# Conditional residual matmul on one core: VectorE multiplies half of the masks in while it evicts, and the first unit's x comes staged

## The chip, the cores and the metric

One Trainium2 chip, one of its cores. The time is the device time of one execution in microseconds (us), lower is better. All data is float32.

## The reference, cut to what matters

```python
# x (128, 128, 512), y = cond_8 (128, 8), weight (8, 512, 512), mask (512, 512), bias (512,)
masked_w = weight * mask[None, :, :]
w_bot = jnp.einsum('bg,got->bot', y, masked_w)      # one 512x512 matrix for each batch b
x = x + jnp.einsum('bnt,bot->bno', x, w_bot) + bias
```

Each of the 128 batches has its own matrix `w_bot[b]`, a sum of eight masked matrices weighted by `y[b]`. It is made on the chip, then multiplied with `x[b]`, and the input and a bias are added.

## The kernel before

**Units.** The work is cut into 8 units: 2 slices of 256 output columns, times 4 windows of 32 batches. A unit has 16 bursts (16 output rows `o` of the mask each), which make `w_bot` of its window and slice in `wbot`, and jobs, which multiply x with `wbot` and leave sums in a PSUM bank. 16 groups of 2 batches make up a unit. While a unit's jobs run, the bursts of the next unit run between them; only the first 8 bursts of the program (`HALF`) stand alone at the start.

**A burst** (`burst(b)`, L528) is 16 matmuls, 4 row tiles `j` by 4 parts `k` of t. The stationary operand is `wm`, weights that were multiplied by the mask; the moving one is `y_sb`, a blocked table of y. Row tiles run beside each other on 32 rows of the array each. Each row tile fills a bank of its own. Each of these four tiles is evicted from PSUM to its place in `wbot`: ScalarE takes tiles 0 and 2 (`ACT.Copy`, L363), VectorE tiles 1 and 3 (`tensor_copy`, L440), by `on_vector` (L156).

**x itself.** In unit 0 the residual x is added by TensorE: each burst has four further bf16 matmuls (`add_x`, L539) of the 0/1 table `eye_sb`, which add the identity to `w_bot`. `AHEAD` says which bursts have them first and which last. In the other units x comes from DRAM a second time, laid out like the output (`xn`), into the six buffers `staged`; VectorE adds the bias to it (L458) and then the sums (`add_sums`, L476). In unit 0 `add_sums` adds the bias straight to the sums.

**Masks.** The weights of a slice lie in `wm`, 16 blocks of 256 KB, and each block is multiplied by an equally large block of mask (`multiply_mask`, L278): for slice 0 by VectorE for blocks 0, 1 and 3 and by GpSimd (POOL) for the others, for slice 1 by POOL alone, while units 2 and 3 run. Masks of slice 0 lie where later x groups go (`first_mask`), so an x group waits for the multiplications that read its place (`masked`, L271). POOL's order is that of the blocks.

**Queues.** SyncE (SP) issues nearly every load in one written order: 8 blocks of weights and masks, two x groups, then pairs of blocks between x groups; later an x group as soon as its ring place is free, `xn` as soon as an output buffer is stored, and from x group 48+2 on the weights and masks of slice 1 (`LOAD_W_AT`). ScalarE's queue issues the first mask, y, the 0/1 table, the bias and all stores. `room` (L515) makes TensorE wait until its bank was evicted (`s_ev_v`, `s_ev_a`) or its sums were added (`s_o`).

**Jobs.** The first jobs of a unit are pieces of all 128 rows (`piece`, L584). Later groups come four jobs at a time in four turns (`turn`, L597) with a burst between turns. In the first half of unit 0 a job takes half of the columns, and two bursts stand ahead of jobs 2, 4, 6 and 7. The banks go round: the third and fourth tile of burst 9 take the banks of job 0 and job 1, so they wait for VectorE's `add_sums` of these.

## Time and profile before

| what | value |
|---|---|
| time, median of 3 runs | 588.47 us (587.61 to 588.82) |
| time of the profiled execution | 590.58 us |
| its span | 588.8 us |
| TensorE (PE) busy | 577.1 us, 98% of the span |
| VectorE (DVE) busy | 328.7 us, 56% |
| ScalarE (ACT) busy | 160.5 us, 27% |
| GpSimd (POOL) busy | 38.4 us, 7% |
| loads and stores | 148.71 MB, 253 GB/s over the span |

The profiled execution took 1.8 us more than its span and 2.1 us more than the median of the three timed runs. A line of the profile names an engine, the line of the kernel, what is written and what is read. PEld is TensorE's weight load, which runs beside the matmuls. A float32 matmul has two records of each kind, so a burst shows as x32, and a turn of 16 matmuls as x32.

### The profile page before, as it was taken

Reading aid. Unit: us, or ns where it says so; the run is one execution under the profiler, and the core shown is the slowest. Engines: PE = TensorE matmul, PEld = TensorE weight load, DVE = VectorE, ACT = ScalarE, POOL = GpSimd, SP = SyncE. Lnnn points to the kernel's source line nnn. Section 1 sums busy time; section 2 is a strip of 40 time slices with the busy share of each in tenths; the row PEclk is TensorE's granted clock in tenths of the full one; section 3 lists DMA queues with packets and bytes.
Section 4 is the critical chain, followed back from the end, with each engine's and each line's share of the span. In section 5 each row is a group of like instructions: output and inputs, shape, how many; then the busy total and the mean of one; then the engine's idle time right before and its main releaser. Section 6 shows DMA issues by size and latency. Waiting matters only on the chain.

```text
span 588.8 us, 20669 instructions
## 1 busy us (share of the span) xinstructions
PE 577.1 (98%) x9148; PEld 542.0 (92%) x9148; DVE 328.7 (56%) x600; ACT 160.5 (27%) x334; POOL 38.4 (7%) x34
## 2 busy tenths in 40 slices
PE   7899999999999999999999999999999999999998
PEld 4799999889998999989899899998999989999887
DVE  5562557346673476645666356663566635665333
ACT  5340444014440144302343023430234203441000
POOL 3430000000000011123110000000000000000000
PEclk9999999999999999999999999999999999999999
DMA  9978546884668869899676875769676795759842
GB/s 320 407 298 287 179 147 216 288 332 154 220 216 306 282 199 326 264 351 411 244 269 223 313 267 164 258 187 349 201 216 212 226 339 185 243 172 313 273 159 89
DMA packets 59849, 148.71 MB, mean 253 GB/s; under 512 B 6624, under 2 KB 7520, under 8 KB 59760
## 3 DMA queue, kind: packets, MB, share of 16 engines
q1 hardware_dynamic: 40176, 113.00, 57.4%
q10 hardware_dynamic: 19584, 34.39, 15.4%
q8 instruction: 72, 1.18, 0.8%
q14 instruction: 17, 0.14, 0.1%
HBM read 113.81 MB, written 33.55 MB: 250 GB/s over the span
## 4 chain that ended last, share of the span: by engine, by line
PE 96%; DMA 1%; issue 1%; POOL 1%; SPq 1%; DVE 0%; DVEq 0%; POOLq 0%
PE ps L592 43%; PE ps L611 34%; PE ps L562 19%; DMA xs<-in_mask 1%; POOL wm L284 1%; SPq L307 0%; SPq L313 0%; PE ps L545 0%; DVE wbot L440 0%; DVE staged L476 0%; DVEq L474 0%; POOLq L282 0%
## 5 line engine op out<-in xcount | busy, mean ns | idle before, releaser
L592 PE MATMUL ps<-wbot,xs 128*128 128x256 f32 (+1 forms) x1400 | 253.7, 343 | 0.8 <-DVE wbot L440 0.8
L592 PEld LDWEIGHTS ps<-wbot,xs 128*128 128x128 f32 x1400 | 227.1, 191 | 25.4 <-issue 1.6
L363 ACT ACTIVATE wbot<-ps 128x512 f32<-128x512 f32 (+2 forms) x277 | 140.8, 567 | 343.0 <-PE ps L562 337.1
L611 PE MATMUL ps<-wbot,xs 32*128 32x256 f32 x3584 | 220.9, 376 | 0.1
L440 DVE COPY wbot<-ps 128x512 f32<-128x512 f32 (+2 forms) x274 | 164.6, 646 | 93.2 <-PE ps L562 89.6
L611 PEld LDWEIGHTS ps<-wbot,xs 32*128 32x128 f32 x3584 | 188.1, 185 | 2.6 <-issue 1.0
L562 PEld LDWEIGHTS ps<-y_sb,wm 32*128 32x128 f32 x4096 | 144.8, 186 | 11.4 <-issue 7.0
L562 PE MATMUL ps<-y_sb,wm 32*128 32x128 f32 x4096 | 147.9, 273 | 5.9 <-issue 4.3
L476 DVE TENSOR_TENSOR staged<-ps,staged 128x256 f32<-128x256 f32 (+2 forms) x121 | 63.9, 544 | 140.5 <-PE ps L592 127.2
L458 DVE TENSOR_TENSOR staged<-staged,bias_sb 128x512 f32<-128x512 f32 (+2 forms) x121 | 79.3, 661 | 0.0
L284 POOL TENSOR_TENSOR wm<-wm,mask_sb 128x512 f32<-128x512 f32 x16 | 21.3, 1354 | 243.4 <-DMA mask_sb<-in_mask 243.4
L400 ACT ACTIVATE eye_sb<-ps 128x256 f32<-128x256 f32 x56 | 18.5, 381 | 25.1 <-PE ps L611 25.1
L476 DVE TENSOR_TENSOR staged<-ps,bias_sb 128x256 f32<-128x256 f32 x24 | 9.8, 423 | 19.2 <-PE ps L592 15.7
L476 DVE TENSOR_TENSOR staged<-eye_sb,staged 128x256 f32<-128x256 f32 x48 | 18.0, 417 | 0.1
L284 POOL TENSOR_TENSOR wm<-wm,xs 128x512 f32<-128x512 f32 x13 | 16.4, 1271 | 21.9 <-DMA xs<-in_mask 21.8
L619 PE MATMUL ps<-staged 128*128 128x512 f32 x4 | 3.6, 1047 | 1.4 <-DVE staged L478 1.4
L545 PE MATMUL ps<-eye_sb 32*128 32x128 bf16 x64 | 3.6, 219 | 1.0 <-DMA eye_sb<-in_eye 0.8
L284 DVE TENSOR_TENSOR wm<-wm,xs 128x512 f32<-128x512 f32 x3 | 2.1, 689 | 4.1 <-DMA xs<-in_mask 4.1
L545 PEld LDWEIGHTS ps<-eye_sb 32*128 32x128 bf16 x64 | 1.8, 93 | 2.2 <-DMA eye_sb<-in_eye 1.0
L619 PEld LDWEIGHTS ps<-staged 128*128 128x128 f32 x4 | 1.2, 324 | 2.5 <-DVE staged L478 1.4
L476 DVE TENSOR_TENSOR staged<-eye_sb,bias_sb 128x256 f32<-128x256 f32 x8 | 3.0, 417 | 0.0
L363 ACT ACT_TABLE_LOAD x1 | 1.3, 1283 | 3.2 <-issue 3.2
(6 smaller groups left out, 1.5 us busy)
## 6 DMA issues: line engine op xcount, KB each, us to landing
xs<-in_x SPq DMA_DIRECT2D x128, 512.0 KB, 5.4
out<-staged ACTq DMA_DIRECT2D x127, 256.0 KB, 5.1
staged<-in_xn SPq DMA_DIRECT2D x112, 256.0 KB, 3.9
wm<-in_w SPq DMA_DIRECT2D x12, 512.0 KB, 8.5
mask_sb<-in_mask SPq DMA_DIRECT2D x8, 512.0 KB, 7.5
wm<-in_w SPq DMA_DIRECT2D x8, 256.0 KB, 5.9
xs<-in_mask SPq DMA_DIRECT2D x4, 512.0 KB, 13.0
xs<-in_mask SPq DMA_DIRECT2D x7, 256.0 KB, 6.3
```

The lines of the kernel that those rows point to most:

```text
L284: return eng.tensor_tensor(wm[:, c, :], wm[:, c, :], by, ALU.mult)
L363: eng.activation(tile_place(b, j, first, end), tile_sums(b, j, first, end), ACT.Copy).then_inc(s_ev_a, 1)
L400: eng.activation(late_of(i), ps[BANK_OF[i, None]][:, 0:SL], ACT.Copy).then_inc(s_late, 1)
L440: eng.tensor_copy(tile_place(b, j, first, end), tile_sums(b, j, first, end)).then_inc(s_ev_v, 1)
L458: ins = eng.tensor_tensor(at, at, bias_of(i, at.shape[1]), ALU.add)
L476: eng.tensor_tensor(at, total, at if m >= OWN_X else bias_of(i, at.shape[1]), ALU.add).then_inc(s_o, 1)
L545: ins = eng.matmul(bank[j][:, own * P:(own + 1) * P], eye_sb[rows[j], c % (P // CO), :], ones_sb[rows[j], :], start=ahead, stop=behind)
L562: ins = eng.matmul(bank[j][:, k * P:(k + 1) * P], wm[rows[j], c, k * P:(k + 1) * P], y_sb[rows[j], win, :], start=not (ahead and k == own) ...
L592: ins = eng.matmul(bank[:, at:at + width], group[:, h, k, :], sums_of(slice(0, P), u, g, h, c, end, k), start=(k == 0), stop=(k == KT - 1))
L611: ins = eng.matmul(ps[BANK_OF[i, None]][:, 0:WIDTH[i]], xs[rows, X_AT[u, g] % XRING, h, k, :], sums_of(rows, u, g, h, c, end, k), start=(n ...
L619: eng.matmul(ps[BANKS - 1][:, :], staged[:, 0, 0:P], staged[:, 0, :], start=True, stop=True)
```

## The change

**Half of the masks move to the eviction.** Weights now lie in pairs of blocks, rearranged on the host so that the even block of a pair holds all rows that ScalarE evicts and the odd block all rows that VectorE evicts (`block_of`). ScalarE takes tiles 0 and 1 of even bursts and 2 and 3 of odd ones, VectorE the other two (`on_vector`). Only even blocks are multiplied by a mask, block 0 by VectorE and the rest by POOL. VectorE evicts with `tensor_tensor`, which multiplies the sums from PSUM by the table `factor_sb` (mask values, 64 for each row tile, the same for all groups of batches). The table is 512 KB for a slice: for slice 0 in two halves of 256 KB, for slice 1 in one, issued at x group 58 after VectorE's last eviction of slice 0.

**Unit 0 is like the others.** `add_x`, the 0/1 table and its four loads are gone (64 bf16 matmuls). `xn` and its bias addition now begin with output tile 0: 16 further loads of 256 KB and 16 further additions on VectorE.

**Small things.** The masks of slice 0 lie in ring places 6 to 9, so x groups 2 to 5 wait for nothing. y is loaded one unit at a time into two buffers, by ScalarE's queue. The bias is issued one burst earlier. The multiplied block of slice 1 needs one mask buffer of 256 KB.

```diff
-    return j == 3 or j == 1 and b not in BY_VECTOR[:2]
+    return j // 2 != b % 2
+def block_of(c, j):
+    return c - c % 2 + (j // 2 != c % 2)
-BY_VECTOR = (0, 1, 3)
-BY_POOL = tuple(_c for _c in range(CS) if _c not in BY_VECTOR)
+BY_VECTOR = (0,)
+BY_POOL = tuple(_q for _q in range(PAIRS) if _q not in BY_VECTOR)
+LOAD_FACTOR_AT = LAST_UNIT + 10
...
+        def multiply_mask(eng, s, q):
+            eng.wait_ge(s_w[2 * q], 16 * (s + 1))
+            eng.wait_ge(s_mask[q], 16 * (s + 1))
+            by = mask_sb[:, :] if s else first_mask[:, q, :]
+            return eng.tensor_tensor(wm[:, 2 * q, :], wm[:, 2 * q, :], by, ALU.mult)
+        def factor_of(b, j, count):
+            at = j % 2 * KT * GB * TO
+            return factor_sb[:, b % CS, at:at + KT * GB * TO].rearrange(
+                "p (a o) -> p a o", o=TO).unsqueeze(2).to_broadcast([P, KT * GB, count, TO])
...
+                if m == 0:
+                    eng.wait_ge(s_s1, 1)
+                elif m >= OUTB:
+                    stored(eng, m - OUTB)
                 eng.dma_start(staged_of(m), xn[m]).then_inc(s_xn[m % OUTB], 16)
...
-                        eng.tensor_copy(tile_place(b, j, first, end), tile_sums(b, j, first, end)).then_inc(s_ev_v, 1)
+                        if b in (0, HALF):
+                            eng.wait_ge(s_factor[b // HALF], 16)
+                        elif b == WINDOWS * CS:
+                            eng.wait_ge(s_factor[0], 32)
+                        eng.tensor_tensor(tile_place(b, j, first, end), tile_sums(b, j, first, end),
+                                          factor_of(b, j, end - first), ALU.mult).then_inc(s_ev_v, 1)
...
             multiply_mask(eng, 0, 0).then_inc(s_mul_v, 1)
             for b in range(HALF):
-                if b + 1 in BY_VECTOR:
-                    multiply_mask(eng, 0, b + 1).then_inc(s_mul_v, 1)
                 evict(b)
+            biased = bias_up_to(0)
...
-                eng.tensor_tensor(at, total, at if m >= OWN_X else bias_of(i, at.shape[1]), ALU.add).then_inc(s_o, 1)
+                eng.tensor_tensor(at, total, at, ALU.add).then_inc(s_o, 1)
...
+                for k in range(KT):
+                    for j in range(TILES):
+                        rows = slice(j * TR, (j + 1) * TR)
+                        bank = room((b, j)) if k == 0 else ps[BANK_OF[b, j]]
+                        ins = eng.matmul(bank[:, k * P:(k + 1) * P], wm[rows, block_of(c, j), k * P:(k + 1) * P],
+                                         y_sb[rows, u % 2, :], start=True, stop=True)
```

On VectorE at the start of the program, before. `x8` means eight in a row; L284 multiplies by the mask, L440 evicts (`128x8x3x4` and `128x8x13x4` are the two parts of a tile of bursts 6 and 7), L476 adds the sums of a job:

```order
L284 TENSOR_TENSOR wm<-wm,xs 128x512 [waits s_mask1,s_w1]
L440 COPY wbot<-ps 128x8x16x4 [waits s_s1] x2
L284 TENSOR_TENSOR wm<-wm,xs 128x512 [waits s_mask3,s_w3]
L440 COPY wbot<-ps 128x8x16x4 [waits s_s1] x8
L440 COPY wbot<-ps 128x8x3x4 [waits s_s1] x4
L440 COPY wbot<-ps 128x8x13x4 [waits s_s1] x4
L476 TENSOR_TENSOR staged<-ps,bias_sb 128x256 [waits s_s2,s_bias]
L476 TENSOR_TENSOR staged<-ps,bias_sb 128x256 [waits s_s2]
L440 COPY wbot<-ps 128x8x16x4 [waits s_s1] x4
```

VectorE at the same place now, where L469 evicts, L490 adds the bias to x and L503 adds the sums:

```order
L469 TENSOR_TENSOR wbot<-ps,factor_sb 128x8x16x4 [waits s_factor0,s_s1] x2
L469 TENSOR_TENSOR wbot<-ps,factor_sb 128x8x16x4 [waits s_s1] x10
L469 TENSOR_TENSOR wbot<-ps,factor_sb 128x8x3x4 [waits s_s1] x4
L469 TENSOR_TENSOR wbot<-ps,factor_sb 128x8x13x4 [waits s_s1] x4
L490 TENSOR_TENSOR staged<-staged,bias_sb 128x512 [waits s_xn0,s_bias]
L503 TENSOR_TENSOR staged<-ps,staged 128x256 [waits s_s2,s_xb]
L490 TENSOR_TENSOR staged<-staged,bias_sb 128x512 [waits s_xn1]
L503 TENSOR_TENSOR staged<-ps,staged 128x256 [waits s_s2,s_xb]
L469 TENSOR_TENSOR wbot<-ps,factor_sb 128x8x16x4 [waits s_factor1,s_s1] x2
```

Two mask multiplications left VectorE, two evictions of the first bursts came to it from ScalarE, and the additions of jobs 0 and 1 now stand behind waits for `xn` 0 and 1.

SP's loads around the first x groups, before (128x512 is 256 KB, 128x1024 is 512 KB):

```order
L313 DMA xs<-in_mask 128x512
L322 DMA xs<-in_x 128x1024 x2
L307 DMA wm<-in_w 128x1024
L313 DMA xs<-in_mask 128x1024
L322 DMA xs<-in_x 128x1024 [waits s_mul_v]
L322 DMA xs<-in_x 128x1024 [waits s_mul_v,s_mul_p]
L307 DMA wm<-in_w 128x1024
L313 DMA xs<-in_mask 128x1024
```

And now:

```order
L309 DMA wm<-in_w 128x512 x2
L326 DMA xs<-in_x 128x1024 x2
L334 DMA staged<-in_xn 128x512 [waits s_s1]
L312 DMA xs<-in_mask 128x512
L309 DMA wm<-in_w 128x1024
L316 DMA factor_sb<-in_factor 128x512
L326 DMA xs<-in_x 128x1024 x2
L334 DMA staged<-in_xn 128x512
L312 DMA xs<-in_mask 128x512
```

Ahead of the first x groups there are 3 masks on this queue where there were 7. Behind them, `xn` 0 and 1 and the second half of the factor table came in, and each mask is half as large.

## Rows read from the trace of the kernel before

**Rows 1.** The page: busy time, and the forty slices of clock and DMA.

```profile
PE 577.1 (98%) x9148; PEld 542.0 (92%) x9148; DVE 328.7 (56%) x600; ACT 160.5 (27%) x334; POOL 38.4 (7%) x34
PEclk9999999999999999999999999999999999999999
```

**Rows 2.** The page: chain that ended last, by engine.

```profile
PE 96%; DMA 1%; issue 1%; POOL 1%; SPq 1%; DVE 0%; DVEq 0%; POOLq 0%
```

**Rows 3.** Timeline of the start, several engines: start us, us, instructions, [idle before].

```profile
5.56 1.17 PE L562 MATMUL ps<-y_sb,wm 32*128 32x128 f32 x32 [0.54 <-DMA y_sb<-in_yblk]
8.22 1.27 POOL L284 TENSOR_TENSOR wm<-wm,xs 128x512 f32<-128x512 f32 x1 [6.92 <-DMA xs<-in_mask]
10.83 5.31 DVE L440 COPY wbot<-ps 128x512 f32<-128x512 f32 x8 [0.60 <-PE ps L545]
10.93 3.97 POOL L284 TENSOR_TENSOR wm<-wm,xs 128x512 f32<-128x512 f32 x3 [1.43 <-DMA xs<-in_mask]
16.04 1.27 POOL L284 TENSOR_TENSOR wm<-wm,xs 128x512 f32<-128x512 f32 x1 [1.14 <-DMA xs<-in_mask]
19.32 3.81 PE L592 MATMUL ps<-wbot,xs 128*128 128x128 f32 x32 [0.77 <-DVE wbot L440]
21.67 2.50 POOL L284 TENSOR_TENSOR wm<-wm,xs 128x512 f32<-128x512 f32 x2 [4.37 <-DMA xs<-in_mask]
22.51 0.42 DVE L476 TENSOR_TENSOR staged<-ps,bias_sb 128x256 f32<-128x256 f32 x1 [1.48 <-DMA bias_sb<-in_bias]
```

**Rows 4.** Busy time by stretch, 18 to 26 us: DMA share and GB/s last.

```profile
18.00:20.00 2.00, 1.23 (x26) 1.07 (x23) 1.39 (x5) 1.61 (x7) 0.00 (x0) 1.00 1.03 405
24.00:26.00 2.00, 2.00 (x53) 1.67 (x46) 1.68 (x3) 1.61 (x4) 0.18 (x1) 1.00 1.05 418
```

**Rows 5.** Timeline of the first jobs: restart of the jobs after bursts 8 and 9, POOL.

```profile
25.39 3.84 PE L592 MATMUL ps<-wbot,xs 128*128 128x128 f32 x32
26.79 2.50 POOL L284 TENSOR_TENSOR wm<-wm,xs 128x512 f32<-128x512 f32 x2 [2.62 <-DMA xs<-in_mask]
32.55 2.49 POOL L284 TENSOR_TENSOR wm<-wm,xs 128x512 f32<-128x512 f32 x2 [3.26 <-DMA xs<-in_mask]
37.07 2.51 POOL L284 TENSOR_TENSOR wm<-wm,xs 128x512 f32<-128x512 f32 x2 [2.03 <-DMA xs<-in_mask]
40.84 0.11 PEld L545 LDWEIGHTS ps<-eye_sb 32*128 32x128 bf16 x4
41.10 16.34 PE L592 MATMUL ps<-wbot,xs 128*128 128x128 f32 x144
```

**Rows 6.** Units 1 to 3 by stretch: us, busy PE, PEld, DVE, ACT, POOL, clock, DMA.

```profile
100.17:171.09 70.92, 70.92 (x1170) 67.57 (x1169) 41.77 (x77) 20.15 (x43) 0.00 (x0) 1.00 0.71 240
171.09:244.03 72.94, 71.35 (x1170) 67.39 (x1169) 41.49 (x77) 20.02 (x43) 7.92 (x6) 1.00 0.81 275
244.03:317.90 73.87, 72.37 (x1169) 67.67 (x1169) 43.95 (x77) 20.05 (x44) 13.38 (x10) 1.00 0.83 298
```

**Rows 7.** Waits from 200 to 318 us: waited for, us in total, times, longest.

```profile
PEld ps L562 <- issue: 4.3, 6, 1.5
```

**Rows 8.** The page: instruction queue of the DMA engines.

```profile
q8 instruction: 72, 1.18, 0.8%
```

**Rows 9.** Groups by form: busy us, mean ns, idle before.

```profile
L440 DVE COPY wbot<-ps 128x512 f32<-128x512 f32 x234 | 150.5, 686 | 91.2 <-PE ps L562 88.9 <-PE ps L545 1.6
L476 DVE TENSOR_TENSOR staged<-ps,staged 128x512 f32<-128x512 f32 x56 | 38.7, 692 | 125.9 <-PE ps L592 125.9
L458 DVE TENSOR_TENSOR staged<-staged,bias_sb 128x512 f32<-128x512 f32 x104 | 73.2, 704 | 0.0
```

**Rows 10.** Timeline, 226 to 229 us: VectorE's evictions and the next burst's weight loads.

```profile
227.34 1.29 DVE L440 COPY wbot<-ps 128x512 f32<-128x512 f32 x2 [0.73 <-PE ps L562]
228.55 0.62 PEld L562 LDWEIGHTS ps<-y_sb,wm 32*128 32x128 f32 x13
```

**Rows 11.** Timeline around 286 us: a bias addition beside POOL.

```profile
285.62 2.50 POOL L284 TENSOR_TENSOR wm<-wm,mask_sb 128x512 f32<-128x512 f32 x2 [8.49 <-DMA mask_sb<-in_mask]
286.98 1.68 DVE L458 TENSOR_TENSOR staged<-staged,bias_sb 128x512 f32<-128x512 f32 x1
```

216 lines of the change are left out of this document (94 added, 122 removed).

## The prediction

> **What bounds the kernel now.** I read the page first: TensorE is busy for 98% of the span and its clock row is 9 in all forty slices [rows 1], and the chain that ended last is TensorE for 96% [rows 2]. VectorE, at 56%, and the DMA engines are off it on average. So two things can move the time: TensorE's own work, and the few places where it stands still. The timeline of the start and the comparison of the units give these places.
>
> The first is the start. The first job begins at 19.32 us, released by VectorE's eviction [rows 3]. Ahead of it stand eight bursts, and these follow the masks: POOL multiplies at 8.22, 10.93 and 16.04 us, each time just after a mask landed [rows 3]. The DMA engines are full there, share 1.03 to 1.05, 405 to 418 GB/s [rows 4]. From 19.3 us on TensorE hardly stands still in unit 0.
>
> The second is units 2 and 3. From the first job of one unit to that of the next, unit 1 takes 70.92 us, unit 2 72.94 and unit 3 73.87, with DMA shares of 0.71, 0.81 and 0.83 [rows 6]. These two units carry the loads for slice 1. The excess is 2.02 + 2.95 = 5.0 us. The waits name no releaser but "issue": 4.3 us in 6 pieces for the bursts' weight loads [rows 7]. TensorE's own instructions come through the DMA engines too, 72 packets of 1.18 MB together, so 16 KB each [rows 8]. I take the holes for late instruction loads: they stand in the middle of bursts, where no semaphore is waited for, and only where the DMA engines carry the most.
>
> **The start, with the new order of loads.** I count what SP's queue has issued in blocks of 256 KB and read from the old trace when a block is there to be used. Old order: the mask of burst 2 is block 5 and used at 8.22 us; block 9 at 10.93, block 15 at 16.04, block 23 (masks 8 and 9) at 21.67 [rows 3]; block 31 at 26.79, block 39 at 32.55, block 45 at 37.07 [rows 5]. ScalarE's queue carries 220 KB more at the start now (factor table for the 0/1 table), which I count as 0.86 block ahead of all. In the new order the weights of pair 1 complete block 4, of pair 2 block 7, of pair 3 block 10, of pair 4 block 19, `xn` 1 is block 25, pair 5 ends at 28, `xn` 2 is 33, pair 6 ends at 36, pair 7 at 42. Interpolated, with 0.86 added, these are there at 8.1, 10.2, 12.5, 19.5, 23.5, 25.4, 28.9, 31.0 and 35.5 us. A POOL multiplication takes 1.27 us [rows 3], so the masked blocks are ready at 9.4, 11.4, 13.8, 20.7, 26.7, 32.3 and 36.7 us.
>
> Now VectorE becomes the pace of the start. Burst 0 can begin at 5.56 us as before. A tile is ready some 1.2 us after its burst's start (the burst lasts 1.17 us, rows 3). The factor table must be there as well; estimated from its place behind mask 0 and y on ScalarE's queue, it lands near 6.9 us. Eight evictions in a row took 5.31 us, 0.66 each [rows 3]. Two tiles of each burst: bursts 0 and 1 are out at 9.5; burst 2 starts at 9.4, and bursts 2 and 3 are out at 13.3; bursts 4 and 5 (masked at 11.4) are out at 15.9; burst 6, started at 14.6, gives its short parts at 16.35; burst 7 needs the bank that is free at 15.9 and gives its short parts at 17.5. The first job starts at 17.7, not at 19.32: a gain of 1.6 us. The bounds are 17.3 (no instruction load in the way) and 18.8 (one hole of about 1.1 us, as units 2 and 3 have them).
>
> **Then the staged x takes most of that back.** Jobs 0 and 1 take 3.81 us [rows 3], to 21.5. Bursts 8 and 9 have their weights at 20.7. But the fourth tile of burst 9 takes the bank of job 1, so it waits for VectorE's addition of job 1, and that now stands behind the bias addition to `xn` 1, there at 23.5. 0.65 us for this addition and 0.42 for the sums (22.51 us row of rows 3) make 24.6. The rest of the burst, 13 of 16 matmuls, is about 0.9 us: jobs 2 and 3 start at 25.5, where they started at 25.39 [rows 5]. The bias itself (issued a burst earlier, and 1.48 us late before at 22.51, rows 3) is no longer last. So the 1.6 us are gone by job 2, and the new wait is 2 to 3 us long inside burst 9. Between 25.39 and 41.10 the 0/1 matmuls of six bursts fall away, 0.10 us each (four weight loads take 0.11, rows 5): 0.6 us. Later weights are in time: pair 5 ready at 26.7, wanted at 29.3; pair 6 at 32.3, wanted near 35; pair 7 at 36.7, wanted near 39. Job 7 starts 0.5 us earlier than before. If `xn` 1 lands at 22.7 or 24.7, this is 1.3 earlier or 0.7 later; if it were no bar at all, TensorE's own path would make it 1.6 + 0.6 = 2.2 earlier. I take -0.5.
>
> One rule of the chip speaks against this place. At 286.98 us a bias addition, both inputs in SBUF, took 1.68 us beside POOL's multiplication, 1.0 more than its usual 0.68, while the addition from PSUM at 22.51 kept its 0.42 beside POOL's row at 21.67 [rows 3, 11]. The Trainium skill has this as a rule (SBUF — State Buffer, "Who interferes with whom"): a VectorE instruction with two SBUF inputs is blocked by a GpSimd instruction that reads SBUF, one with a single SBUF input is not. The trace agrees. The new evictions have one input in PSUM, so they keep their pace; the new bias additions have two in SBUF, but by my times the one that matters (23.5) lies between POOL's multiplications of 19.5 and 25.4, so I charge nothing; a collision would put 1.0 us on burst 9.
>
> **Sixteen more `xn` loads and bias additions.** 4 MB more in unit 0, 2 MB less masks. After 41 us they are hidden: units 1 and 4 to 6 carry the same and take 70.92 us with TensorE always busy [rows 6]. VectorE has 16 x 0.70 = 11 us more work over some 80 us, as in those units. If that cover were gone, the price would be an addition of 0.7 us for a tile. I take 0.
>
> **Evictions by multiplication.** A copy of a tile takes 686 ns on the mean; the nearest row is the addition from PSUM and SBUF of the same size, 692, and the one from SBUF alone 704 [rows 9]. So 6 to 18 ns more each; below nothing I see no reason for. What hides this is the turn between two bursts, and there the room is small: VectorE ends its pair at 227.34 + 1.29 = 228.63, and the next burst's weight loads begin at 228.55 and reach the fourth tile some 0.13 later [rows 10]. With the new split VectorE has tiles 2 and 3 of even bursts, the last two to be wanted, and of odd bursts tiles 0 and 1, ready first but wanted first. There are 12 such handovers in a unit, 6 from an even burst, 42 in the seven units that have them. Room is about 0.02 to 0.05 us at the even ones. I take 0.3 us in all, with 0 and 1.3 as ends (42 x 0.03).
>
> **The slice-1 loads.** 16 weight blocks and 16 mask blocks were loaded in units 2 and 3; now 16, 8 and 2 for the factor table, 26 in place of 32. POOL has 8 multiplications in place of 16. The holes of 5.0 us should shrink more than the traffic, since they come only at the top of it; instruction loads are also shifted by the missing matmuls, which makes single holes a matter of luck. I take a gain of 1.5 us, with 0.5 lost and 4.0 gained as ends.
>
> **Other edits.** The later y loads (64 KB each) are issued a unit ahead and wait for bursts long done; the wait ahead of the factor table on SP, with x and `xn` behind it, is for an eviction of the start of unit 3, over when x group 58 may be loaded. 0.
>
> **Sum.** -0.5 (start) + 0.3 (evictions) - 1.5 (slice 1) = -1.7 us. On the profiled execution: 590.58 becomes 588.9, its span 588.8 becomes 587.1. The profiled one is 2.1 us above the median of the three runs, and I take the difference off the median: 588.47 - 1.7 = **586.8 us**.
>
> **Rivals.**
> - **Staged x in time and holes gone.** If `xn` 1 lands before 21.5, the start keeps 2.2 us, and if the lower traffic takes 2.5 of the 5.0 us, the time is 588.47 - 2.2 - 2.5 = 583.8. For it: SP no longer holds back x groups 2 to 5, so the queue is never short. Against it: the DMA engines are full already [rows 4], so bytes decide.
> - **The holes stay.** If the holes don't hang on how much is loaded, units 2 and 3 keep their 5.0 us and the time is 588.47 - 0.5 + 0.3 = 588.3, no change. For it: "issue" names no cause [rows 7]. The Trainium skill (Runtime: NRT & Kernel Launch, "Instruction fetch mechanics") says that instructions come in blocks of 16 KiB through a queue of the engine's own and that this is normally hidden behind their issue; the packet size agrees [rows 8], but that all is hidden no row shows. Against it: four units without the slice's loads have no holes.
> - **The multiplying eviction is slower, and every handover waits.** Its operand is read in runs of four with a broadcast over groups, which no row shows. From 10 to 25 ns more a tile it decides at even bursts. At 60 ns more, a pair is 0.12 longer: 0.10 x 42 + 0.02 x 42 = 5.0 us more, 588.47 - 2.0 + 5.0 = 591.5, slower. Against it: additions of the same size keep 692 [rows 9], and the copies write the same scattered places.
>
> **How the numbers follow.** Forecast 0.45, staged x in time 0.2, holes stay 0.2, slow evictions 0.15. The forecast's own spread (585.6 to 588.4) puts 0.34 below 587.3, which is 0.2% under the median, and 0.11 within. 0.2% is about what a measurement of this kernel can tell from no change. So faster 0.54, within 0.2% 0.31, slower 0.15. The range goes down to the second case. With every unknown of the forecast at its bad end (+0.7 for the start, +1.3 for the evictions, +0.5 in units 2 and 3) the time would be 591.0; I go up to 589.6, about where two of the three are bad, which also takes in the case of the holes. 583.8 to 589.6 leaves out the slow evictions and a little below the second case.
>
> **What would show it.** The first job at 17.7 (start); a wait inside burst 9 before jobs 2 and 3 at about 25.5, with `xn` 1's bias addition at about 23.5; job 7 near 40.6; L469's mean between 692 and 704 ns; unit 1 still at 70.9 and units 2 and 3 together at 145.3 in place of 146.8. The prediction is wrong if unit 1 is longer than 71.5 (evictions on the path), if jobs 2 and 3 start before 24 or after 27, or if units 2 and 3 don't move or lose their whole excess.

## The result, and the profile after

The changed kernel is slower by half a per cent: 591.08 us, median of 20 runs (587.70 to 596.07), against 588.66 us (586.11 to 590.74, 20 runs) for the kernel before on the same chip. The ratio is 1.0047, with a 95% interval of 1.0027 to 1.0067. The prediction was 586.8 us, faster, with 589.6 as the upper end of its range: the time lies above the range, and the difference to the kernel before is clear of the noise in the other direction. The profiled execution of the changed kernel took 591.91 us, its span 589.9.

The page of the changed kernel, busy time, clock row and the chain that ended last:

```profile
PE 578.9 (98%) x9084; PEld 544.1 (92%) x9084; DVE 337.4 (57%) x616; ACT 159.5 (27%) x332; POOL 20.0 (3%) x19
PEclk9999999999999999999999999999999999999999
PE 95%; DMA 3%; issue 1%; SPq 0%; DVE 0%; ACTq 0%; DVEq 0%
```

POOL went from 38.4 to 20.0 us and VectorE from 328.7 to 337.4, as the change says. TensorE still bounds the kernel, and DMA has 3% of the chain where it had 1% [rows 2], most of it for `xn` (2% in the page's list by line). The start shows where. Its timeline, changed kernel, engine by engine (columns as in [rows 3]):

```profile
5.80 9.85 PE L567 MATMUL ps<-y_sb,wm 32*128 32x128 f32 x216 [0.57 <-DMA y_sb<-in_yblk]
16.99 1.40 PE L567 MATMUL ps<-y_sb,wm 32*128 32x128 f32 x40 [1.34 <-issue]
18.41 2.41 DVE L469 TENSOR_TENSOR wbot<-ps,factor_sb 128x96 f32<-128x96 f32 x6 [0.39 <-PE ps L567]
19.14 3.81 PE L594 MATMUL ps<-wbot,xs 128*128 128x128 f32 x32 [0.74 <-ACT wbot L388]
20.74 0.90 DVE L490 TENSOR_TENSOR staged<-staged,bias_sb 128x512 f32<-128x512 f32 x1
23.84 0.69 DVE L490 TENSOR_TENSOR staged<-staged,bias_sb 128x512 f32<-128x512 f32 x1 [1.75 <-DMA staged<-in_xn]
24.45 0.42 DVE L503 TENSOR_TENSOR staged<-ps,staged 128x256 f32<-128x256 f32 x1
24.93 1.15 PE L567 MATMUL ps<-y_sb,wm 32*128 32x128 f32 x26 [0.66 <-DVE staged L503]
```

TensorE stands still in the middle of burst 6 for 1.34 us, to 16.99, and waits for no semaphore. The first job comes at 19.14, hardly earlier than the 19.32 of before. Then `xn` 1 is late: VectorE idles for 1.75 us to 23.84, and the rest of burst 9 waits for it. Jobs 2 and 3 start at 26.01, where they started at 25.39 [rows 5].

The stretches from the first job of a unit to that of the next, units 1 to 3, changed kernel (columns as in [rows 6]):

```profile
102.00:172.67 70.67, 70.67 (x1172) 67.13 (x1169) 41.63 (x77) 20.11 (x42) 0.00 (x0) 1.00 0.72 241
172.67:246.44 73.77, 71.62 (x1172) 67.63 (x1169) 42.86 (x78) 20.07 (x42) 4.39 (x3) 1.00 0.80 264
246.44:317.65 71.21, 71.11 (x1172) 67.17 (x1169) 42.23 (x77) 20.10 (x42) 6.54 (x5) 1.00 0.85 300
```

Unit 1 takes 70.67 us, 0.25 less than in this trace of before (a second trace of before, below, has 70.69). Units 2 and 3 take 144.98 together where they took 146.81. So in this one trace the slice-1 term of the sum seems right. The evictions and bias additions of a full tile, changed kernel, by form (busy us, mean ns, idle before):

```profile
L469 DVE TENSOR_TENSOR wbot<-ps,factor_sb 128x512 f32<-128x512 f32 x236 | 151.4, 685 | 83.4 <-PE ps L567 82.2
L490 DVE TENSOR_TENSOR staged<-staged,bias_sb 128x512 f32<-128x512 f32 x120 | 83.0, 692 | 2.2 <-DMA staged<-in_xn 2.2
```

An eviction that multiplies takes 685 ns, the copy took 686 [rows 9].

Unit 1 starts at 102.00 in the changed kernel and at 100.17 before [rows 6], 1.8 us later, of which 0.4 is there at burst 16, the first between turns (57.79 against 57.38). So the rest was lost in the second half of unit 0. The timeline of its weight loads has a hole there, where the trace of before has none:

```profile
77.72 3.10 PEld L613 LDWEIGHTS ps<-wbot,xs 32*128 32x128 f32 x57 [0.92 <-issue]
```

The 20 runs fall into two groups. In 11 the mean granted clock was 1.0 (median 589.5 us), in 9 it was 0.997 (median 593.4). The profiled execution is one of the first group, so its page can't show the second. In the tables below one run of kernel e6 (595.17 us) counts as slow, 1.5% above the fastest of that kernel, and its ratio leaves it out.

### The profile page after: what moved, and what is told of

Read it like the earlier page. It is cut to its first block, busy times and chain, and to the rows that moved or that the text cites. A ratio compares the mean times of both kernels' runs of the same rounds, so it can differ in the third digit from the quotient of the medians.

```text
span 589.9 us, 20560 instructions
## 1 busy us (share of the span) xinstructions
PE 578.9 (98%) x9084; PEld 544.1 (92%) x9084; DVE 337.4 (57%) x616; ACT 159.5 (27%) x332; POOL 20.0 (3%) x19
## 4 chain that ended last, share of the span: by engine, by line
PE 95%; DMA 3%; issue 1%; SPq 0%; DVE 0%; ACTq 0%; DVEq 0%
PE ps L594 42%; PE ps L613 34%; PE ps L567 19%; DMA staged<-in_xn 2%; DMA y_sb<-in_yblk 1%; DVE staged L503 0%; SPq L326 0%; SPq L312 0%; SPq L316 0%; SPq L309 0%; ACTq L407 0%; SPq L334 0%; DVEq L466 0%; DVE staged L490 0%; DVEq L501 0%
## 5 line engine op out<-in xcount | busy, mean ns | idle before, releaser
L469 DVE TENSOR_TENSOR wbot<-ps,factor_sb 128x512 f32<-128x512 f32 (+2 forms) x276 | 165.4, 646 | 85.5 <-PE ps L567 84.3
L503 DVE TENSOR_TENSOR staged<-ps,staged 128x256 f32<-128x256 f32 (+2 forms) x145 | 73.6, 523 | 158.4 <-PE ps L594 140.3
L567 PEld LDWEIGHTS ps<-y_sb,wm 32*128 32x128 f32 x4096 | 147.2, 188 | 11.6 <-issue 6.7
L567 PE MATMUL ps<-y_sb,wm 32*128 32x128 f32 x4096 | 149.9, 276 | 5.2 <-issue 3.8
L490 DVE TENSOR_TENSOR staged<-staged,bias_sb 128x512 f32<-128x512 f32 (+2 forms) x137 | 89.1, 655 | 2.2 <-DMA staged<-in_xn 2.2
L427 ACT ACTIVATE late_sb<-ps 128x256 f32<-128x256 f32 x56 | 18.6, 381 | 24.4 <-PE ps L613 24.4
L503 DVE TENSOR_TENSOR staged<-late_sb,staged 128x256 f32<-128x256 f32 x56 | 21.8, 430 | 0.0
L284 POOL TENSOR_TENSOR wm<-wm,mask_sb 128x512 f32<-128x512 f32 x8 | 10.9, 1366 | 254.7 <-DMA mask_sb<-in_mask 254.7
L284 POOL TENSOR_TENSOR wm<-wm,xs 128x512 f32<-128x512 f32 x7 | 8.9, 1273 | 28.1 <-DMA wm<-in_w 28.1
L284 DVE TENSOR_TENSOR wm<-wm,xs 128x512 f32<-128x512 f32 x1 | 0.7, 692 | 3.5 <-DMA xs<-in_mask 3.5
```

The source lines that it names most:

```text
L284: return eng.tensor_tensor(wm[:, 2 * q, :], wm[:, 2 * q, :], by, ALU.mult)
L427: eng.activation(late_of(i), ps[BANK_OF[i, None]][:, 0:SL], ACT.Copy).then_inc(s_late, 1)
L469: eng.tensor_tensor(tile_place(b, j, first, end), tile_sums(b, j, first, end), factor_of(b, j, end - first), ALU.mult).then_inc(s_ev_v, 1)
L490: ins = eng.tensor_tensor(at, at, bias_of(i, at.shape[1]), ALU.add)
L503: eng.tensor_tensor(at, total, at, ALU.add).then_inc(s_o, 1)
L567: ins = eng.matmul(bank[:, k * P:(k + 1) * P], wm[rows, block_of(c, j), k * P:(k + 1) * P], y_sb[rows, u % 2, :], start=True, stop=True)
```

## The experiments

Each kernel is set against the kernel before on the same chip: e1 to e4 on one chip, e5 to e8 on a second and e9 to e12 on a third, where the means of before are 589.16, 588.92 and 588.86 us, so the chips themselves differ by 0.3 us at most. The changed kernel's first 20 runs stand against 20 of before (mean 588.50), for which no clock is on record; they are not among the 93. "Clock below 1" counts the runs whose mean granted clock was 0.997 or 0.994. Start is the start of the first job, burst 16 that of the first burst between turns, both in the one profiled execution.

| kernel | runs | median us | mean us | ratio, 95% | clock below 1 | start | burst 16 | to unit 1 | units 2+3 |
|---|---|---|---|---|---|---|---|---|---|
| before, on three chips | 93 | 589.38, 589.21, 588.70 | 588.98 | 1 | 9 of 93 | 19.29 | 57.38 | 42.72 | 146.81 |
| before again (e5) | 12 | 588.79 | 588.69 | 0.9977 to 1.0010 | 1 | 19.62 | 57.52 | 42.73 | 143.68 |
| changed | 20 | 591.08 | 591.54 | 1.0027 to 1.0067 | 9 | 19.10 | 57.79 | 44.21 | 144.98 |
| changed again (e1) | 12 | 592.54 | 592.33 | 1.0024 to 1.0072 | 8 | 19.40 | 58.58 | 44.48 | 143.78 |
| copy in the eviction (e2) | 12 | 592.05 | 592.67 | 1.0034 to 1.0077 | 7 | 18.60 | 57.81 | 43.50 | 145.61 |
| `xn` first (e3) | 12 | 590.12 | 589.69 | 0.9986 to 1.0030 | 0 | 19.02 | 56.57 | 42.72 | 146.17 |
| `xn` first again (e10) | 12 | 589.39 | 589.51 | 0.9995 to 1.0030 | 0 | 19.32 | 56.86 | 42.78 | 142.95 |
| staged x alone (e4) | 6 | 593.86 | 594.01 | 1.0042 to 1.0094 | 6 | 17.92 | 61.79 | 43.20 | 144.67 |
| `xn` first, x held (e6) | 12 | 589.77 | 590.10 | 0.9988 to 1.0039 | 4 | 19.38 | 58.56 | 43.02 | 148.07 |
| 64 waits ahead (e7) | 12 | 590.76 | 591.02 | 1.0009 to 1.0056 | 7 | 20.14 | 58.40 | 42.95 | 144.63 |
| no slice-1 loads (e8) | 12 | 586.46 | 586.63 | 0.9947 to 0.9979 | 2 | 17.98 | 56.18 | 43.21 | 141.71 |
| `xn` first, filled (e9) | 12 | 588.42 | 588.71 | 0.9966 to 1.0017 | 2 | 19.10 | 56.65 | 42.73 | 146.22 |
| changed, burst 9 filled (e11) | 6 | 592.66 | 592.41 | 1.0038 to 1.0080 | 4 | 18.33 | 59.85 | 43.63 | 141.99 |
| changed, filled (e12) | 12 | 589.72 | 589.69 | 1.0001 to 1.0030 | 2 | 18.79 | 58.13 | 44.15 | 144.69 |

"To unit 1" is the time from burst 16 to the first job of unit 1; start, burst 16 and the units are read from the weight loads, so they stand some hundredths ahead of the matmul rows. An undisturbed unit takes 70.67 or 70.68 us in every kernel but one (the shortest unit with staged x alone took 70.82), so units 2 and 3 would take 141.35 together.

### The changed kernel again, and the kernel before again

> The changed kernel once more, unaltered, as the anchor on this chip. In its first profile the wait inside burst 9 cost 0.9 us, one hole in unit 0's turns 0.9 and units 5 and 6 together 2.1 more than two undisturbed units (70.67 us each). Theory A (holes in TensorE's instruction supply come at random, more often where the DMA engines carry more): median 1.5 to 3.5 us above the kernel before, a spread of 5 us or more, holes of 0.5 to 1.5 us at other places than in the first profile. Rival B (a fixed cost per burst or per handover): units 1 and 4 longer than 70.9 us, spread as in the kernel before.

> The kernel before once more, unaltered, for a second trace of it. Its first trace lost 6.5 us over six undisturbed units (70.67 us each) in units 1 to 6, of them 5.5 in units 2 and 3. Theory A (holes in TensorE's instruction supply): again a start near 19.3 us with a hole of about 1 us inside burst 6 that the mask wait hides, a loss of 3 to 6 us in units 2 and 3 and under 1.5 in the others; ratio 1.

The slowdown repeats: 1.0048, with a spread of 7.5 us and units 1 and 3 at 70.68 and 70.67 us, so it is no fixed cost for each burst. With the clock below 1 in 8 of 12 runs, the low clock of the first runs was no accident. This profiled execution is one of those, and its stretches show where (columns as in [rows 6]):

```profile
18.00:19.00 1.00, 0.69 (x27) 0.50 (x20) 0.61 (x4) 0.76 (x4) 0.00 (x0) 1.00 1.07 404
19.00:23.00 4.00, 3.57 (x18) 3.60 (x19) 3.28 (x6) 1.41 (x5) 1.27 (x1) 0.59 1.04 400
23.00:27.00 4.00, 4.00 (x81) 3.76 (x81) 2.43 (x5) 1.01 (x3) 0.68 (x1) 0.99 1.03 404
```

The granted clock is 0.59 on the mean of 19 to 23 us: 3.41 us at level 0.5, from 19.7, that is 1.2 GHz in place of 2.4. TensorE's weight loads had stood still for 1.8 us in burst 6, from 15.48. Jobs 0 and 1 took 5.44 us in this trace where they take 3.81 at full clock, so the fall costs 1.6 us there; 3.41 us at half speed can take at most 1.7. The Trainium skill (TensorE: Matmul & The Clock Gate, "Part 1: The HAM clock gate (the "warmup" mystery)") says that the gate has only two levels and goes to the lower one when TensorE has been idle; the traces here show only 1.0 and 0.5, and each fall before the end of TensorE's work came after an idle piece, in the start or, in one case, at 303 us. These idle pieces were some 1 to 5 us long and ended at the fall or up to 2.4 us before it; pieces of over 1 us brought none in other executions.

The second trace of before was the more sobering one. Its units 2 and 3:

```profile
170.94:242.90 71.96, 70.93 (x1172) 67.25 (x1169) 41.59 (x77) 20.01 (x43) 7.50 (x6) 1.00 0.80 273
242.90:314.62 71.72, 71.61 (x1171) 67.71 (x1169) 43.21 (x77) 20.05 (x44) 13.11 (x10) 1.00 0.87 314
```

That is 143.68 us for the same instructions that took 146.81 in the first trace [rows 6]. The excess over 141.35 is 2.3 us in one and 5.5 in the other. A single trace can't carry a term that is smaller than this scatter.

### The eviction as a copy

This kernel leaves out the multiplication in VectorE's evictions and does everything else.

```diff
-    eng.tensor_tensor(tile_place(b, j, first, end), tile_sums(b, j, first, end),
-                      factor_of(b, j, end - first), ALU.mult).then_inc(s_ev_v, 1)
+    eng.tensor_copy(tile_place(b, j, first, end), tile_sums(b, j, first, end)).then_inc(s_ev_v, 1)
```

> The changed kernel, in which VectorE copies its tiles instead of multiplying them by the factor table (all loads, also the table's, stay; the output lacks the masks of VectorE's rows). If the multiplying eviction costs time: 1 us or more faster than the changed kernel. Theory A: the same as the changed kernel within its spread, and the mean of an eviction of a whole tile within 10 ns of it.

Its evictions of full tiles, by form:

```profile
L469 DVE COPY wbot<-ps 128x512 f32<-128x512 f32 x236 | 151.4, 686 | 83.5 <-PE ps L566 80.8 <-DMA factor_sb<-in_factor 2.0
```

686 ns again, and a median of 592.05, between the changed kernel's two (591.08, and 592.54 on this chip; means 592.7 and 592.3 on this chip). A gain of 1 us or more is not there: the multiplication costs nothing that these runs can tell, either in VectorE's time or at the handovers.

### xn 1 ahead of its x groups

```diff
                     load_factor(0, 1)
+                load_xn(q - PAIRS // 2 + 1)
                 for n in range(n, n + (2 if q < PAIRS - 2 else 1)):
                     load_x(n)
                 n += 1
-                load_xn(q - PAIRS // 2 + 1)
```

> The changed kernel, with each staged-x load of the start issued ahead of the x groups that it followed. Staged x 1 is four 256 KB blocks earlier in the queue, so it lands about 2.5 us earlier, at 21.3 in place of 23.8. My step on burst 9: the wait inside burst 9 (0.85 us) vanishes and jobs 2 and 3 start at 25.0 to 25.3 in place of 26.0; the time falls by 0.7 to 1.0 us. Rival: x groups 2 and 3 then land late and the wait only moves, no gain.

> xn 1 ahead of its x groups, the same kernel as once before, beside the one with 56 further instructions. Theory: 589.0 to 590.6 as before, no or at most 2 of 12 runs with a clock below 1.0; hole in burst 6 again 1.0 to 1.6 us, first job 18.8 to 19.3; single holes in units 2 and 3 stand at other places than in its first trace if they are a matter of timing, at the same places within 2 us if they hang on the count of instructions. Rival (0 of 12 was luck): 4 or more of 12 runs with a fallen clock.

The start in the second of these traces, TensorE and VectorE:

```profile
17.20 1.40 PE L567 MATMUL ps<-y_sb,wm 32*128 32x128 f32 x40 [1.35 <-issue]
19.34 3.81 PE L594 MATMUL ps<-wbot,xs 128*128 128x128 f32 x32 [0.74 <-ACT wbot L388]
22.01 0.68 DVE L490 TENSOR_TENSOR staged<-staged,bias_sb 128x512 f32<-128x512 f32 x1
23.09 2.07 PE L567 MATMUL ps<-y_sb,wm 32*128 32x128 f32 x64
25.08 3.17 PE L594 MATMUL ps<-wbot,xs 128*128 128x128 f32 x26
```

The bias addition to `xn` 1 now runs at 22.01, bursts 8 and 9 are one piece, and jobs 2 and 3 start at 25.08, though the hole in burst 6 is as long as before. Three things went together: the wait in burst 9, the low clock (none of 24 runs, against 17 of the 32 of the changed kernel), and the loss in the second half of unit 0 (42.72 and 42.78 us, against 44.21 and 44.48). The mean of the 24 runs is 589.6 us, 2.2 under the mean of 591.8 of the 32. That is more than the 0.7 to 1.0 us expected of the wait alone. Against the kernel before it is level; neither measurement can tell the ratio from 1. The edit moves four loads, `xn` 1 to 4, each ahead of the x groups of its place; only `xn` 1 was waited for in the start.

The holes in units 2 and 3 are not the same in the two traces, and the two units went from 146.17 to 142.95 us. The first has holes of over 0.4 us that end at 227.5, 239.1, 299.2 and 310.4 us, the second one at 237.6. So timing decides whether there is a hole; at which instructions there can be one is another matter (below).

### Staged x alone

All masks multiplied in ahead, as in the kernel before, with unit 0's x staged. (The other half alone can't be had in this form: the identity that TensorE adds in unit 0 would be multiplied by the mask at the eviction.)

```diff
-                ahead, behind = b in AHEAD, u == 0 and b not in AHEAD
-                if ahead:
-                    add_x()
...
-                eng.tensor_tensor(at, total, at if m >= OWN_X else bias_of(i, at.shape[1]), ALU.add).then_inc(s_o, 1)
+                eng.tensor_tensor(at, total, at, ALU.add).then_inc(s_o, 1)
```

> The kernel before with only the staged x of unit 0 (no 0/1 table, sixteen more staged loads and bias additions); masks, evictions and y as before. If the staged x is the cost: slower than the kernel before by 1.5 us or more, as the changed kernel, with holes in unit 0's turns and a wait inside burst 9 of about 2 us (staged x 1 is block 28 there, landing near 25). If the masks' part or the y loads are the cost: within 1 us of the kernel before plus that wait.

The timeline of TensorE in this kernel, and its stretch of 27 to 30 us (columns as in [rows 6]):

```profile
24.01 2.19 PE L537 MATMUL ps<-y_sb,wm 32*128 32x128 f32 x38 [2.24 <-POOL wm L277]
26.90 2.07 PE L537 MATMUL ps<-y_sb,wm 32*128 32x128 f32 x26 [0.71 <-DVE staged L471]
28.90 3.27 PE L564 MATMUL ps<-wbot,xs 128*128 128x128 f32 x17
```

```profile
27.00:30.00 3.00, 3.00 (x31) 2.77 (x32) 2.33 (x4) 1.09 (x2) 1.51 (x2) 0.50 1.04 406
```

The first job is early, 17.95, but with full masks and `xn` in the same queue TensorE waits 2.24 us for block 8 and again for the sums of job 1, and the clock is at 0.5 from 24.4 to 31.2 us. Jobs 2 and 3 start at 28.90. The median is 593.86 us, and all 6 runs have a clock below 1. So staged x, in this order of loads, is the part that costs, and the half masks give back some 2.2 us of its 5.0 (means 594.0 and 591.8, before 589.0).

### Why the first job is late

Three kernels go at the hole in burst 6. TensorE's instructions come in packets of 16 KB [rows 8]; the first of the span was on its queue from 14.62 to 15.73 us in the changed kernel, and TensorE went on at 16.99. The eight traces with half masks and the same instructions ahead of burst 6, from the records of packets and weight loads (us):

| kernel | packet moved at | hole ends | its length | first job |
|---|---|---|---|---|
| e8 | 14.52 | 15.87 | 0.67 | 17.98 |
| e11 | 14.90 | 16.22 | 0.89 | 18.33 |
| e2 | 15.23 | 16.48 | 1.17 | 18.60 |
| e3 | 15.48 | 16.91 | 1.26 | 19.02 |
| changed | 15.73 | 16.99 | 1.53 | 19.10 |
| e10 | 15.77 | 17.20 | 1.54 | 19.32 |
| e6 | 15.69 | 17.27 | 1.53 | 19.38 |
| e1 | 16.03 | 17.29 | 1.81 | 19.40 |

The hole ends 1.3 to 1.6 us after the packet, and the first job starts 2.11 or 2.12 us after the hole in all eight. So the hole sets the start.

It is not only this hole. The 14 traces have 63 holes of more than 0.4 us in TensorE's weight loads that no semaphore ends, from burst 5 on (the wait of the first job for its evictions, which that view calls "issue" too, left out). Every one ends 1.1 to 1.6 us after an instruction packet was moved, though such stretches of half a microsecond make up only some 6% of the span. And counted in TensorE's instructions (both records of a matmul, and its waits), the places of all 63 differ by whole multiples of 256, within 1 (the kernel before has some 18,500 of these instructions and 72 packets, 256 for each). That holds for the holes in the second half of unit 0 and in units 2 and 3 alike. They are places where a new packet begins, and the packet was late.

The first of the three kernels tests whether the long queue of x loads delays that packet. It has `xn` first and holds x groups 4 and 5 until masks 3 and 4 are multiplied in:

```diff
+                elif n in (4, 5):
+                    masked(eng, 0, n - 1)
```

> As the third experiment (staged x ahead of its x groups), and SP's queue holds x groups 4 and 5 back until masks are multiplied, as the kernel before did. Theory C: the hole inside burst 6 comes from the deeper DMA queue of the changed kernel, behind which TensorE's instruction packet waits; then the packet starts at 13.8 or earlier in place of 14.5, and the first job starts at 18.4 or earlier in place of 19.0, the time falls by about 0.6. Rival: the packet's time does not hang on what is queued, and nothing moves.

Its TensorE:

```profile
17.27 1.40 PE L569 MATMUL ps<-y_sb,wm 32*128 32x128 f32 x40 [1.34 <-issue]
19.41 5.44 PE L596 MATMUL ps<-wbot,xs 128*128 128x128 f32 x32 [0.74 <-ACT wbot L390]
24.77 2.07 PE L569 MATMUL ps<-y_sb,wm 32*128 32x128 f32 x64
```

Theory C gets no support: the hole is 1.53 us in weight loads, the packet starts at 14.66 and the first job at 19.38. But the test is weak. x group 4 was issued at 13.94 all the same, since mask 3 was multiplied in by then, so only x group 5 and what follows it were missing from the queue when the packet started. Whether a much shorter queue would bring the packet sooner isn't shown. The clock fell in 4 of 12 runs, in this one at 19.70, although bursts 8 and 9 are one piece: here the hole of burst 6 is the longest idle piece behind the start of burst 0.

The second moves the packet's boundary with 128 written waits ahead of burst 0 (64 instructions), on top of `xn` first:

```diff
+            for _ in range(128):
+                eng.wait_ge(s_zeros, 1)
             for b in range(HALF):
```

> As the third experiment, with 64 further waits on a semaphore that is long set, in TensorE's stream behind the two warm-up matmuls: all that follows lies a quarter of a 16 KB instruction packet further on. Theory A: the hole of burst 6 moves back by 64 instructions (one burst), into burst 5, and all later holes change place and size, so the loss in units 1 to 6 differs by 1 us or more from the third experiment's. Rival (the holes belong to places of the work): they stay in burst 6 and in the same turns.

Its timeline has one row for TensorE's bursts:

```profile
8.48 10.98 PE L567 MATMUL ps<-y_sb,wm 32*128 32x128 f32 x256 [3.29 <-issue]
```

The eight bursts are one piece, without a hole, but the waits themselves held burst 0 until 8.48. So there is no hole in burst 5, as theory A had it: with everything behind the waits 2.4 us later, the packet (13.77 to 14.84) was there before TensorE wanted it. The later holes did move, as the theory said: the one that the changed kernel, e1 and e10 have at weight load 8454 stands at 8422 here, 32 weight loads or 64 instructions of bursts and jobs earlier. From burst 0 to the first job it takes 11.7 us, where the changed kernel takes 13.3 (5.80 to 19.10). Taken from the changed kernel's start of burst 0, that would be a first job at 17.5 (an estimate: here the masks were early and the clock was low for a part). The prediction counted 12.1 us from burst 0. The clock was low from 8.4 us on for 3.41 us, after the idle time in front, and fell in 7 of 12 runs.

The third fills TensorE's wait for the masks ahead of burst 2 with 14 matmuls (56 instructions) into banks that burst 2 overwrites. It was run with `xn` first and with the changed kernel's order:

```diff
+                if b == 2:
+                    for n in range(14):
+                        j = n % TILES
+                        rows = slice(j * TR, (j + 1) * TR)
+                        eng.matmul(room((b, j))[:, 0:P], wm[rows, block_of(0, j), 0:P],
+                                   y_sb[rows, 0, :], start=True, stop=True)
                 if win == 0:
                     masked(eng, s, c // 2)
```

> xn 1 ahead of its x groups, and 14 further matmuls (56 TensorE instructions) between burst 1 and burst 2, where TensorE waits for the masks anyway. They write to banks that burst 2 overwrites. Theory (the start is late because TensorE's instructions come too late, and a packet is asked for when TensorE has got through an earlier one): the earlier packet boundary now falls before burst 2's wait for its mask, so the packet whose lateness made the hole in burst 6 comes about 1 to 2 us earlier than TensorE's place moves forward. The hole in burst 6 (1.1 to 1.8 us) is at most 0.5, the first job starts at 17.8 to 18.4 instead of 19.0, and the median is 588.6 to 589.6, about 0.8 us under the kernel with xn 1 first alone; no clock fall in any run. Rival (the packet comes at its time whatever TensorE did): hole and start as before, or the hole is longer by 0.9 because the boundary is reached earlier, and the time equals that kernel's or is 0.5 to 1 longer.

> The changed kernel with the 14 further matmuls between bursts 1 and 2, xn 1 in its place. Theory 1 (the clock falls after the hole in burst 6): the hole is at most 0.5 us, and the clock falls in at most 2 of 12 runs; the wait for xn 1 in burst 9 is longer by what the start gains (1.5 to 2.5 us), jobs 2 and 3 start at 25.5 to 26.0, and the median is 589.0 to 590.3. Rival (the clock falls because of the wait in burst 9): half of the runs or more fall, since the wait is longer, with the fallen stretch behind 24, as in the kernel with staged x alone, median 591 to 593. Rival 2 (the hole doesn't go): all as in the changed kernel.

The changed kernel with the filling:

```profile
15.56 2.70 PE L573 MATMUL ps<-y_sb,wm 32*128 32x128 f32 x68 [0.58 <-issue]
18.82 3.81 PE L600 MATMUL ps<-wbot,xs 128*128 128x128 f32 x32 [0.56 <-ACT wbot L388]
25.26 1.15 PE L573 MATMUL ps<-y_sb,wm 32*128 32x128 f32 x26 [1.31 <-DVE staged L503]
26.34 1.83 PE L600 MATMUL ps<-wbot,xs 128*128 128x128 f32 x14
```

The hole is 0.58 us here (0.77 in weight loads, in both filled kernels) and ends at 15.56, not 16.99. It is another place of the work: the 14 matmuls moved it by 27 weight loads, from burst 6 into the end of burst 5, so that 68 matmul records stand behind it where 40 stood. The packets started at 12.97 and 13.30, where those of the eight traces above started at 13.42 to 14.92; that fits the theory that instructions got through earlier bring the next packet earlier, with two traces for it. The first job is no earlier: 18.79, with 18.33 to 19.40 in the four traces of the changed order of loads, and 19.10 with `xn` first, where 17.8 to 18.4 was expected. But the low clock is rare: 2 of 12 runs in place of 17 of 32, although the wait in burst 9 is twice as long (1.31 us); with `xn` first it is 2 of 12 too, where none was expected. The mean is 589.7 us, 2.1 under the changed kernel's, with no step of the start gained. About half of that is the low clock: among runs at clock 1 the means are 589.4 and 590.5. The other half these runs don't explain.

With `xn` first the filled kernel has the lowest median of those that do all the work, 588.42 us, but its ratio to the kernel before, 0.9966 to 1.0017, is no difference.

### The wait in burst 9 filled

Four matmuls on one row tile ahead of the wait for job 1's bank, in the changed kernel:

```diff
+                        if b == HALF + 1 and (k, j) == (0, TILES - 1):
+                            for _ in range(4):
+                                eng.matmul(ps[BANK_OF[b, 2]][:, 3 * P:4 * P], wm[2 * TR:3 * TR, block_of(c, 2), 0:P],
+                                           y_sb[2 * TR:3 * TR, u % 2, :], start=True, stop=True)
```

> The changed kernel with four matmuls on one row tile inside burst 9, just ahead of the wait for the bank of job 1, written to a place that burst 9 overwrites. Each should take 0.2 to 0.3 us, so they fill 0.8 to 1.2 us of the wait and cost 0 to 0.4. Theory 1 (the clock falls after the idle piece of the start, the hole in burst 6): this changes nothing, about half of the runs have a fallen clock, median 590.5 to 592.5. Rival (the clock falls because of the wait in burst 9): no fall or at most 2 of 12, median 589.3 to 590.3.

Its timeline, and its stretches behind burst 9:

```profile
20.55 1.69 DVE L490 TENSOR_TENSOR staged<-staged,bias_sb 128x512 f32<-128x512 f32 x1 [0.50 <-DMA bias_sb<-in_bias]
23.34 1.05 PE L568 MATMUL ps<-y_sb,wm 32*128 32x128 f32 x8
25.38 1.15 PE L571 MATMUL ps<-y_sb,wm 32*128 32x128 f32 x26 [0.99 <-DVE staged L503]
```

```profile
23.00:27.00 4.00, 3.01 (x54) 2.70 (x47) 2.70 (x5) 1.64 (x4) 0.71 (x1) 0.93 1.03 402
27.00:30.00 3.00, 3.00 (x17) 3.00 (x16) 0.72 (x2) 0.53 (x2) 0.57 (x1) 0.53 1.02 401
```

The four matmuls took 1.05 us, and 0.99 of the wait was left, since this execution began its first job early, at 18.36. So the wait was shortened but not taken away, and the rival isn't tested cleanly. The low clock stayed, in 4 of 6 runs. In this trace it comes behind burst 9, from 26.4 us on, and not at 19.7 as in the other. So the first job's hole isn't the only idle piece that can bring it. Both the filling ahead of burst 2 and `xn` first made it rarer; which idle piece decides in a given execution stays open, and no run here separates it further.

### Slice 1 without its loads

With `xn` first, and without the weights, masks and factors of slice 1 and POOL's multiplications of them: units 4 to 7 multiply with slice 0's weights.

```diff
-                if n in LOAD_W_AT:
-                    q = LOAD_W_AT[n]
-                    eng.wait_ge(s_s1, ((WINDOWS - 1) * CS + 2 * q + 2) * TILES)
-                    load_blocks(1, 2 * q, 2)
...
-                if n == LOAD_FACTOR_AT:
...
-            for s in range(SLICES):
+            for s in range(1):
                 for q in range(PAIRS) if s else BY_POOL:
```

> As the third experiment, but weights, masks and factor table of slice 1 are not loaded and not multiplied (slice 0's are used again, so the output of the other half is not the reference's). My step on slice 1: the loads are the cause of the loss in units 2 and 3; then these units take 70.7 to 71.2 us each, and the time falls by 3 to 5 us against the third experiment. Rival (holes are luck of the packet's place): units 2 and 3 still lose 2 us or more together.

Its units 2 and 3, and the waits of their bursts' weight loads from 172 to 318 us (waited for, us in total, times, longest):

```profile
170.87:241.90 71.03, 70.98 (x1171) 67.39 (x1169) 41.76 (x78) 20.11 (x42) 0.00 (x0) 1.00 0.73 241
241.90:312.58 70.68, 70.68 (x1172) 67.28 (x1169) 41.49 (x77) 20.11 (x42) 0.00 (x0) 1.00 0.71 239
```

```profile
PEld ps L552 <- issue: 0.7, 2, 0.3
```

The same waits of the changed kernel:

```profile
PEld ps L567 <- issue: 3.0, 4, 1.5
```

Without the loads 0.36 us of excess is left, and the mean is 586.6 us, 3.0 under the kernel with them. So the holes of units 2 and 3 do come from the slice-1 loads (with POOL's multiplications, which went with them), and all of it together is worth about 3 us. They are not the only holes: units 1 and 4 to 6 of this kernel lose 2.7 us without any slice-1 load. (This trace also had a first job at 17.98, with a hole of 0.67 us in burst 6, long before any slice-1 load would be issued. Its start is luck: the packet came some 1 us earlier than in most of the others.)

## Why the prediction was wrong

Two steps failed. The sum put the start at -0.5 us because the first job was to be there at 17.7, without a late packet; the packet was late in every trace, and burst 16 started 0.7 us later than before. And "After 41 us they are hidden" put nothing on the second half of unit 0, where 1.6 us were lost. The slice-1 term, -1.5, was read from a difference that changes by 3 us from trace to trace. The low clock stood in no term.

**The first job, 17.7 with 17.3 to 18.8 as bounds: missed.** It starts at 19.10 and 19.40 in the two traces. The step "one hole of about 1.1 us" stood only as the bad bound, and the value taken had none. It was 1.53 and 1.81 us. The start of before already held that hole. TensorE's timeline, kernel before:

```profile
16.20 1.06 PE L562 MATMUL ps<-y_sb,wm 32*128 32x128 f32 x29 [1.41 <-issue]
```

I had passed over it because a mask landed at the same moment (16.04, [rows 3]) and because "issue" names nothing. With the masks early, this hole became what is late next. All eight traces with half masks and the same instructions ahead of burst 6 have it, 0.7 to 1.8 us long in weight loads, and the two filled ones one of 0.8 in burst 5; of the kernels with half masks only the one with the 64 waits has none. VectorE's pace, on which the 17.7 rested, was right up to the hole. Its evictions of bursts 0 to 5 were to be out at 15.9, and they were out at 15.86:

```profile
9.61 6.25 DVE L469 TENSOR_TENSOR wbot<-ps,factor_sb 128x512 f32<-128x512 f32 x10 [0.34 <-PE ps L567]
17.60 0.42 DVE L469 TENSOR_TENSOR wbot<-ps,factor_sb 128x96 f32<-128x96 f32 x2 [1.74 <-PE ps L567]
```

The short parts of burst 6, predicted for 16.35, then began at 17.60.

**The wait in burst 9: right in its mechanism and nearly in its size.** `xn` 1's bias addition was put at 23.5 and came at 23.84, and 24.32 in the second trace; jobs 2 and 3 at 25.5 came at 26.01 and 26.80. The half microsecond comes from the loads: burst 0 began at 5.80, not 5.56, and SP's queue of loads ran a little behind the interpolation. This wait is what `xn` first took away. Since the first job was late as well, nothing was left to set against it: job 7 starts 0.4 to 1.2 us later than before, where I had it 0.5 earlier.

**POOL's times: right.** Masked blocks were predicted for 9.4, 11.4, 13.8, 20.7, 26.7, 32.3 and 36.7; POOL's multiplications end at 9.5, 11.6, 13.6, 21.1, 27.1, 33.0 and 37.4. Counting blocks in a queue that is full predicts landings within 0.7 us over 30 us.

**"I charge nothing" for a collision of bias additions with POOL: wrong place.** I looked at `xn` 1. The one that met POOL was `xn` 0's: 0.90 us in the profiled execution, 1.24 in the second, 1.69 with burst 9 filled. It ended before job 1's sums were wanted, so it cost nothing on TensorE.

**After 41 us "they are hidden": wrong for the second half of unit 0.** From burst 16 to unit 1 it takes 42.7 us before and 43.5 to 44.5 in the five traces with the changed kernel's order of loads (e1, e2, e11, e12 and its own), each with single holes of 0.3 to 1.2 us between 65 and 88 us. With `xn` first it takes 42.7 to 42.8 in three traces, and 42.9 to 43.2 in its variants (e6, e7, e8); with staged x alone, where `xn` stands behind its x groups too, 43.2. The four holes of over 0.4 us there, at 65.6 to 77.7 us, are late packets like the others. I had compared with units 1 and 4 to 6, where the same loads come in a settled order, and rows 6 show only unit 1 of these. They are not free of holes either: over 70.67 us each, the four lose 1.1 and 0.5 us together in the two traces of before and 2.1 and 1.8 in those of the changed kernel (2.4 or less in the others but e8). That the half of unit 0 is longer goes with the order of the first loads, but why the packets are late more often then is open.

**The low clock: not foreseen.** The page of before has 9 in all forty slices [rows 1], and I took it for given. TensorE is at half speed for 3.41 us (by its mean clock of 0.994 about twice that in one run) in 17 of 32 runs, against 10 of the 105 of before. In the 32, the runs that have it are 2.5 us longer in the mean (593.0 against 590.5), more than the 1.6 us that jobs 0 and 1 lost, so something else goes with it. In other kernels the same difference is anything from 0.0 (64 waits ahead, 7 against 5 runs) to 4.7 (e6, 4 against 8), and 0.5 in before, so it is no fixed price. Nor is it the whole loss: the 15 runs of the changed kernel at clock 1 still take 590.5 us in the mean, 1.5 more than the kernel before. So of the 2.9 us about 1.3 come with the low clock and 1.5 without it.

**Evictions, +0.3: 0.** 685 ns against 686, and unit 1 at 70.67 us. The rival that the multiplying eviction is slower is excluded, by both the row and the kernel with copies.

**Slice 1, -1.5: too small to be told from the scatter.** The excess of units 2 and 3 over 141.35 us is 5.5, 2.3 and 3.3 in the three traces with whole masks (before, e5, e4; mean 3.7). (In e6, 6.7, a fall of the clock at 303 us is part of it.) It is 3.6, 2.4, 4.3, 4.8, 6.7, 3.3, 4.9, 1.6, 0.6 and 3.3 in the ten with half masks (mean 3.6). The mechanism (loads make holes) is shown by the kernel without them. That "four units without the slice's loads have no holes" holds for both traces of the kernel before, but not with staged x: 14 of the 63 long holes stand behind unit 0 and outside units 2 and 3, in ten of the twelve other traces, up to 1.68 us long. The step that failed is that six of 32 blocks less would shrink the holes in more than their proportion, and that the 5.0 us of one trace were the kernel's usual ones. Of the rivals, "the holes stay" was right in its condition; its time was 588.3 because it kept the -0.5 of the start.

**The sum again, from the traces.** Two traces each, means of changed against before: burst 16 is 0.7 us later (58.2 against 57.5), the second half of unit 0 takes 1.6 longer (44.3 against 42.7), and units 1 to 6 take 0.3 longer (429.0 against 428.7). That is 2.6 us, and the means of the runs differ by 2.9 (591.8 of 32 runs, 589.0 of 93). So nearly the whole loss lies in unit 0, and the prediction put a gain of 0.5 there. In units 1 to 6 the two kernels differ by less than their traces do (430.5 and 426.9 before, 429.7 and 428.3 now): units 2 and 3 are 0.9 us shorter, the other four 1.1 longer.
